# First FFN of a fused decoder kernel: the remainder of half of P on VectorE straight from PSUM, the scaling of X on ScalarE, and newly written instruction lists

## The reference, cut to what matters

```
x = layernorm(x + attention(x))                      # 16 heads, causal
x = layernorm(x + mixing(context, context, x))       # 16 heads of 8, a causal long convolution
x = layernorm(x + ffn0(x))                           # the part that the change touches
x = layernorm(x + state_space(x))                    # convolution, gated scan, RMS norm
x = layernorm(x + mixing1(x, context))
x = layernorm(x + ffn1(x))                           # ternary weights, Hadamard transform
```

```
xq = activation_quant(rms_norm(x))        # round(127 / max|x| * x), per token
g  = silu(xq @ sign(W_g).T)               # 256 -> 1024
u  = xq @ sign(W_u).T                     # 256 -> 1024
p  = g * u
y  = p @ sign(W_d).T                      # 1024 -> 256, p isn't quantised
```

## Time and profile before

| | us |
|---|---|
| runs | 695.28, 695.84, 696.39 |
| the profiled execution | 695.4 |
| its span (first to last instruction) | 693.3 |
| TensorE matmul busy | 668.4 (96%) |
| VectorE busy | 605.5 (87%) |
| GpSimd busy | 570.5 (82%) |
| ScalarE busy | 423.5 (61%) |

### The profile page before, as it was taken

The page is one execution under the profiler, slowest core; times in us unless marked ns, Lnnn a source line. Parts: engine busy times, 40 slices in busy tenths (PEclk is TensorE's granted clock), DMA queues, the critical chain, the costliest instruction groups (busy, mean ns, idle before and its releaser), DMA issues. The chain is left out here.

```text
span 693.3 us, 13904 instructions
## 1 busy us (share of the span) xinstructions
PE 668.4 (96%) x4318; PEld 482.1 (70%) x4318; DVE 605.5 (87%) x1329; ACT 423.5 (61%) x692; POOL 570.5 (82%) x750
## 2 busy tenths in 40 slices
PE   8999999999999899998899999999999999999994
PEld 7888888754444577786688888855444477777883
DVE  5988889679999998878899999889999998888774
ACT  1765666721370686976798888830101468888985
POOL 3986988987878699994467889999988989989952
PEclk9999999999999999999999999999999999999998
DMA  8820000000400050000211111122000000000001
GB/s 309 334 107 1 2 2 2 2 1 0 182 0 0 1 213 21 2 2 1 95 62 61 61 62 62 62 75 66 0 0 1 0 1 2 16 17 17 16 17 45
DMA packets 12726, 33.39 MB, mean 48 GB/s; under 512 B 2672, under 2 KB 8048, under 8 KB 11376
## 3 DMA queue, kind: packets, MB, share of 16 engines
q1 hardware_dynamic: 12080, 31.99, 12.5%
q10 hardware_dynamic: 576, 0.53, 0.3%
HBM read 30.35 MB, written 2.16 MB: 47 GB/s over the span
## 5 line engine op out<-in xcount | busy, mean ns | idle before, releaser
L1084 PE MATMUL bank<-XT,win_late 128*128 128x256 f32 x320 | 79.8, 385 | 2.0 <-DVE ss_xc L1269 1.6
L632 DVE TENSOR_REDUCE MIX<-m_pr 128x128 f32<-128x1024 f32 x64 | 76.6, 1206 | 0.4
L1269 DVE SCALAR_TENSOR_TENSOR ss_xc<-bank,cw_late,ss_xc 128x254 f32<-128x254 f32 x144 | 67.7, 477 | 6.2 <-ACT ss_xc L1173 2.7
L577 POOL TENSOR_TENSOR m_kv<-CTXT 128x512 f32<-128x512 f32 x64 | 65.1, 1042 | 7.4 <-PE bank L609 7.2
L577 POOL TENSOR_TENSOR m_kv<-XT,CTXT 128x512 f32<-128x512 f32 x64 | 68.0, 1089 | 1.4 <-PE bank L609 1.4
L607 PE MATMUL bank<-m_kv,toep 128*128 128x512 f32 x128 | 66.3, 600 | 1.2 <-POOL m_kv L577 1.0
L609 PE MATMUL bank<-m_kv,toep 128*128 128x512 f32 x128 | 65.4, 592 | 0.0
L608 PE MATMUL bank<-m_kv,toep 128*128 128x512 f32 x128 | 65.4, 592 | 0.0
L1084 PEld LDWEIGHTS bank<-XT,win_late 128*128 128x128 f32 x320 | 56.7, 190 | 11.9 <-DVE ss_xc L1269 4.3
L1562 PE MATMUL bank<-had_last,f_ht 128*128 128x256 f32 x256 | 59.4, 379 | 0.0
L445 POOL TENSOR_TENSOR at_p<-at_p,at_mx 128x512 f32<-128x512 f32 x44 | 45.0, 1041 | 10.6 <-DVE at_mx L355 10.5
(11 more groups left out here) (255 smaller groups left out, 1946.6 us busy)
## 6 DMA issues: line engine op xcount, KB each, us to landing
MIX<-cum_rows SPq DMA_DIRECT2D x15, 512.0 KB, 3.6
...
```

Source lines behind the costliest of these rows:

```text
L577: m = nc.gpsimd.tensor_tensor(KV[n % 3][:, c, :, :].rearrange("p (b j) i -> p b j i", b=HB), ki, vj, ALU.mult)
L632: nc.vector.tensor_reduce(head(MIX)[:, :, a, bass.ts(h, HB), :], PR[n % 2][:, :, :, :].rearrange("p c (b j) i -> p c b j i", b=HB), op=ALU ...
L1084: m = nc.tensor.matmul(bX[(NU * g + n) % 3][:, 0:GS_], win[:, h, off:off + P], XT[:, h, bass.ts(g, GS_)], start=(h == 0), stop=(h == C - 1))
L1269: m = nc.vector.scalar_tensor_tensor(acc[:, :, sh:S], bank[:, :, 0:S - sh], cw[:, r, n:n + 1], acc[:, :, sh:S], ALU.mult, ALU.add)
```

## The change

It has three parts.

1. The remainder of half 0 of P is computed by VectorE from PSUM: P in the bank minus the rounded P. ScalarE's copy of half 0 and GpSimd's subtraction of half 0 go; for half 1 both stay. The bank of half 0 comes free after VectorE's subtraction.
2. `lift` moves from VectorE to ScalarE as an activation with a scale and a bias column; GpSimd fills the bias column once.
3. All four lists are written anew, those of the attention, the mixers, the state space stage and the second FFN included. Apart from the parts above they hold the same calls.

```diff
-    PMT, = two("pmt", [P, FC, S], n=1)
+    PMT, = two("pmt", [P, FC // 2, S], n=1)
...
-    columns = ch.sb("f0_columns", [P, 26])
+    columns = ch.sb("f0_columns", [P, 27])
+    rnd = columns[:, 26:27]
...
             pe.wait_ge(s[f"p{k}_made"], n + 1)
-            upto(pe, s[f"p{k}_kept"], 2 * n)
+            upto(pe, s["p1_kept"], 2 * n) if k else upto(pe, s["p0_rest"], n)
...
             if low:
-                pe.wait_ge(s["p_rest"], 2 * n + k + 1)
+                pe.wait_ge(s[f"p{k}_rest"], n + 1)
             else:
-                pe.wait_ge(s[f"p{k}_kept"], 2 * n + 1)
+                pe.wait_ge(s[f"p{k}_kept"], 2 * n + 1 if k else n + 1)
...
-        def keep_p(n, k):
+        def keep_p(n):
...
+            act.wait_ge(s["p1_turned"], n + 1)
+            upto(act, s["p1_rest"], n)
+            nc.scalar.copy(PMT[:, :, :], bP[1][:, :].rearrange("p (r s) -> p r s", r=4)).then_inc(s["p1_kept"], 1)
+
+        def lift(n):
...
+            act.wait_ge(s["scaled"], 2 * n + 2)
+            upto(act, s["q_made"], n - 1)
+            nc.scalar.activation(Z[n % 2][:, :], X[:, n, :], ACT.Identity, scale=SC[n % 2][:, :], bias=rnd).then_inc(s["shifted"], 1)
...
-        def lift(n):
...
-            nc.vector.tensor_scalar(Z[n % 2][:, :], X[:, n, :], SC[n % 2][:, :], ROUND, ALU.mult, ALU.add).then_inc(s["shifted"], 1)
...
+        def rest_p(n):
...
+            dve.wait_ge(s["p0_kept"], n + 1)
+            upto(dve, s["downed"], 4 * n - 1)
+            nc.vector.tensor_tensor(PL[:, 0:4, :], bP[0][:, :].rearrange("p (r s) -> p r s", r=4), PH[:, 0:4, :].bitcast(F32),
+                                    ALU.subtract).then_inc(s["p0_rest"], 1)
...
+            if n == 0:
+                nc.gpsimd.memset(rnd, ROUND)
...
-        def rest_p(n, k):
...
-            pool.wait_ge(s[f"p{k}_kept"], 2 * n + 2)
-            upto(pool, s["downed"], 4 * n - 1 + k)
-            quarter = slice(4 * k, 4 * k + 4)
-            nc.gpsimd.tensor_tensor(PL[:, quarter, :], PMT[:, quarter, :], PH[:, quarter, :].bitcast(F32), ALU.subtract).then_inc(s["p_rest"], 1)
+        def rest_p(n):
...
+            pool.wait_ge(s["p1_kept"], 2 * n + 2)
+            upto(pool, s["downed"], 4 * n)
+            nc.gpsimd.tensor_tensor(PL[:, 4:8, :], PMT[:, :, :], PH[:, 4:8, :].bitcast(F32), ALU.subtract).then_inc(s["p1_rest"], 1)
...
 def gpsimd_order(a, m, f, x, n, g, again):
...
-    a.shift(1, 1); a.shift(1, 2); a.shift(1, 3); a.spread(3); a.shift(2, 0); a.shift(2, 1); a.shift(2, 2); a.shift(2, 3); a.shift(3, 0); a.spread(4)
...
+    a.shift(1, 1); a.shift(1, 2); a.shift(1, 3); a.spread(3); a.shift(2, 0); a.shift(2, 1); a.spread(4); a.shift(2, 2); a.shift(2, 3); a.residual(0)
```

More of the change, by code:

```diff
@@ L810, in round_p @@
             act.wait_ge(s[f"p{k}_turned"], n + 1)
-            upto(act, s["p_rest"], 2 * n - 1 + k if n else 0)
+            upto(act, s[f"p{k}_rest"], n)
             upto(act, s["downed"], 4 * n - 3 + k)
@@ L910, in norm_out @@
             norm(dve, nc, Y2[n % 2], X[:, n, :], MV3[n % 2], RS3[n % 2], s["rstd3"], s["normed3"], n)
[L912 to L913 removed]
+        return calls(add_x=add_x, stats=stats, aggregate=aggregate, norm_x=norm_x, peak=peak, step_size=step_size, quantise=quantise,
+                     multiply=multiply, rest_p=rest_p, add_down=add_down, stats3=stats3, norm_out=norm_out)
     def gpsimd(pool):
@@ new lines, in tensor_order @@
+    m.mix(5); a.context_turn(15); m.mix(6); a.x_turn(10); a.project(15); a.x_turn(11); m.mix(7); m.mix(8); a.x_turn(12); m.mix(9); a.x_turn(13)
+    m.mix(10); a.x_turn(14); m.mix(11); m.mix(12); a.x_turn(15); m.mix(13); m.mix(14); m.mix(15); m.mix(16); m.mix(17); m.mix(18); m.mix(19)
+    m.totals(); m.mix(20); f.mix_turn(0); m.mix(21); f.mix_turn(1); m.mix(22); m.mix(23); m.mix(24); f.mix_turn(2); m.mix(25); m.mix(26)
+    f.mix_turn(3); m.mix(27); m.mix(28); m.mix(29); m.mix(30); f.q_turn(0); m.mix(31); f.gate(0, 1); f.up(0, 1); f.mix_turn(4); f.gate(0, 0)
@@ new lines, in tensor_order @@
+    x.square_sum(14, 11); n.mix(8); x.x_turn(11, 15); x.out_product(14); n.mix(9); x.square_sum(15, 12); n.mix(10); x.x_turn(12, 16)
+    x.out_product(15); n.mix(11); n.mix(12); x.x_turn(13, 16); n.mix(13); x.x_turn(14, 16); n.mix(14); x.x_turn(15, 16); n.mix(15); n.mix(16)
+    n.mix(17); g.mix_turn(0); g.skip(0); n.mix(18); n.mix(19); g.mix_turn(1); g.skip(1); n.mix(20); n.mix(21); g.mix_turn(2); g.skip(2); n.mix(22)
+    n.mix(23); n.mix(24); g.q_turn(0); g.mix_turn(3); g.skip(3); n.mix(25); n.mix(26); n.mix(27); n.mix(28); g.gate(0, 0); g.up(0, 1); g.mix_turn(4)
@@ new lines, in tensor_order @@
+    g.up(0, 0); g.gate(0, 1); g.skip(4); g.q_turn(1); n.mix(29); g.gate(1, 0); g.up(1, 1); g.q_turn(2); g.up(1, 0); g.gate(1, 1); g.mix_turn(5)
+    g.skip(5); g.gate(2, 0); n.mix(30); g.up(2, 1); g.gate(2, 1); g.h_turn(0, 0); n.mix(31); g.q_turn(3); g.up(2, 0); g.transform(0, 0)
+    g.h_turn(0, 1); g.mix_turn(6); g.skip(6); g.gate(3, 0); g.transform(0, 1); g.h_turn(1, 0); g.q_turn(4); g.gate(3, 1); g.mix_turn(7); g.skip(7)
+    g.h_turn(1, 1); g.up(3, 0); g.transform(1, 0); g.transform(1, 1); g.w_turn(0); g.up(3, 1); g.gate(4, 0); g.h_turn(2, 0); g.gate(4, 1)
@@ L2174, in gpsimd_order @@
-    n.mix(26); n.mix(27); g.rstd(2); n.mix(28); g.rstd(3); g.edge(5); n.mix(29); n.mix(30); n.mix(31); g.first(0); g.edge(6); g.second(0); g.rstd(4)
-    g.edge(7); g.first(1); g.second(1); g.rstd(5); g.first(2); g.second(2); g.rstd(6); g.edge(8); g.rstd(7); g.first(3); g.second(3); g.edge(9)
-    g.first(4); g.edge(10); g.second(4); g.rstd3(0); g.rstd(8); g.first(5); g.rstd3(1); g.second(5); g.first(6); g.rstd(9); g.rstd3(2); g.edge(11)
-    g.second(6); g.rstd(10); g.first(7); g.second(7); g.rstd(11); g.edge(12); g.edge(13); g.rstd3(3); g.first(8); g.second(8); g.rstd(12); g.first(9)
@@ new lines, in gpsimd_order @@
+    g.rstd(2); n.mix(28); g.edge(5); n.mix(29); n.mix(30); n.mix(31); g.rstd(3); g.edge(6); g.first(0); g.second(0); g.edge(7); g.rstd(4); g.first(1)
+    g.second(1); g.edge(8); g.rstd(5); g.first(2); g.edge(9); g.second(2); g.rstd(6); g.rstd(7); g.first(3); g.second(3); g.first(4); g.second(4)
+    g.rstd(8); g.edge(10); g.first(5); g.rstd3(0); g.second(5); g.rstd(9); g.edge(11); g.first(6); g.edge(12); g.rstd3(1); g.second(6); g.rstd3(2)
+    g.first(7); g.rstd(10); g.second(7); g.rstd3(3); g.edge(13); g.first(8); g.rstd(11); g.second(8); g.first(9); g.rstd(12); g.second(9); g.rstd3(4)
@@ L2183 @@
+    g.edge(14); g.first(10); g.rstd(13); g.second(10); g.rstd3(5); g.edge(15); g.rstd3(6); g.rstd(14); g.first(11); g.second(11); g.rstd(15)
+    g.first(12); g.second(12); g.rstd3(7); g.first(13); g.second(13); g.rstd3(8); g.first(14); g.second(14); g.rstd3(9); g.rstd3(10); g.rstd3(11)
+    g.rstd3(12); g.rstd3(13); g.rstd3(14); g.rstd3(15)
 AT = ("wqk_in weights_in later_in pool_consts consts proj_in value_in out_in bv_spread bias_made bp_made "
```

622 lines of the change are left out of this document (300 added, 322 removed).

## The result

The changed kernel takes 727.45 us (median of 4, 726.65 to 728.37) against 695.56 on the same chip: a ratio of 1.0457, interval 1.0442 to 1.0473. The forecast was 699.6, range 695.2 to 703.0. The direction was right, the size was wrong by 28 us, and most of what was missed lies in stages for which the prediction had put down nothing. The profiled execution took 727.04 us, its span 725.1.

What follows compares the result with a forecast made beforehand. TensorE was taken to bound the first FFN, VectorE second. 4.9 us lost, less 1.1 recovered, plus 0 gave 3.8; on the profiled 695.4 that is 699.2, with 0.44 for the median 699.6, range 695.2 to 703.0.

Steps and rivals of the forecast that it cites:

- The other orders: Reordered lists outside the first FFN: 0 (0.8 either way) for attention's first scores, 1 us either way for state space.
- the seam: Start of the first FFN behind the mixer, at 226 to 232 us, where all other engines wait for ScalarE.
- The head of line on ScalarE: First FFN's start: four second-FFN weight instructions wait behind the first copy of Q, putting TensorE 4.9 us behind.
- for two such steps: First FFN's start: 0.42 us for two handovers between first Silu, VectorE's product and TensorE's first turn of P.
- the 1.1 taken off as recovered: First FFN: TensorE wins back half of some 2.15 us of its idle time, 1.1 us.
- The operations at nothing: First FFN: moved subtraction and scaling cost nothing beside TensorE's work; bounds 2.15 us gained, 5.1 lost.
- The moved hop of Q: First FFN: Q goes from VectorE to ScalarE and back, hidden because Q is turned a sample ahead of P.
- The relief wins: Rival, first FFN: relieving GpSimd wins 2.15 us and the start 0.8, giving 692.9 us; chance 0.15.
- lost and given back: Rival: 4.9 us lost at the first FFN's start is regained there and in state space, giving 695.9; chance 0.13.
- VectorE becomes the bound: Rival, first FFN: VectorE's added 5.1 us lie on the path, giving 705.8, or 703.3 for half; chance 0.12.
- the four instructions behind the copy: Sign on ScalarE: three of L549 and one of L556 stand behind the first copy of Q.
- 3 to 4 and over 1: Sign: TensorE idles 3 to 4 us before the first turn of P, over 1 before the next gate product.

Runs made afterwards that it cites:

- the first run: The kernel before with the change's first FFN (its operations and lists), all other stages in the order of before: 704.67 us, ratio 1.0142.

## Why the prediction was wrong

**The failed step** is "The other orders": "in the mixers and the second FFN TensorE has no gaps to win", "1 us either way for the state space stage", and 0 within 0.8 for the attention. An engine that is 97% busy has no gaps to win, but each call moved in four lists can open one. The runs put 2.7 (attention), 8.3 (state space stage) and 10.9 us (second FFN) there, 21.9 of 31.9. I had the first scores and the seam read call by call and had read nothing of the two stages that hold most of the rewritten lines. The idea was one-sided too: where TensorE is nearly full a rewriting can win little and lose much. What the new lists did there is known in part only. In the second FFN 7.2 of the 10.9 us were VectorE's sums stretched beside GpSimd and the late scale; 3.7 there, most of the 8.3 of the state space stage and the 2.7 of the attention stay without a cause that an experiment has shown. That the direction came out right is in part luck: the reason given for it carries some 7 of the 31.9 us.

**The head of line on ScalarE** was right in place and timing (8.05 and 11.19 us against 8.06 and 11.27) and mis-sized: 4.9 less 1.1 us forecast, 7.1 measured alone and 6.5 in the changed kernel. Three things are wrong in the term. The path: the first turn of P was taken to wait for the first Silu and VectorE's product (the 0.42 "for two such steps" rests on that), but it waits for the second Silu, whose bank it writes; so the four turns of P and a turn of the mixer's output came behind the wait in place of inside it, and the next gate product started at 242.61, 1.2 us behind the end of the second copy where 0.2 was forecast. TensorE's clock: the work behind the wait ran at 0.50, which is 1.6 us lost in the first run and 2.4 in the changed kernel by the traces. Before has no wait that long inside the program, so the term needed a rival at half clock. And the 1.1 taken off as recovered: the 5.6 us of waiting and 1.6 of clock in the first run make up the 7.1 without it. In the changed kernel the same count is 5.6 and 2.4, 8.0 against 6.5, so there some may have come back; the scatter of those runs doesn't let one say.

**The operations at nothing** was wrong for the lists of before (7.3 for both, 10.9 and 6.3 apart, where my bound for a loss was 5.1), and nearer where the lists were written for them (2.1 together with the rest of the stage's new order). The bound was VectorE's added busy time. The waits in the runs are those of calls that stand behind the added one in VectorE's queue: TensorE waits 9.6 us for the bank of the last product and for Q with the subtraction alone (1.6 for the bank in before). The moved hop of Q that I called hidden is a part of it: 3.3 us of TensorE's waits with the scaling alone.

**The rivals.** "The relief wins" and "lost and given back" are out: the stages after the first FFN only add to the loss. "VectorE becomes the bound" named the right engine for the operations in the old lists, and its 705.8 was still short of the changed kernel's 727.45. No rival said that the rewritten lists could be worse by themselves, although they were the largest part of the diff.

**The signs named in advance.** Right: the four instructions behind the copy, both times after it, GpSimd's fall of 20.4 us over the span (64.11 in the 100 us, near 67 forecast). Wrong: one wait of 5.92 in place of 3 to 4 and over 1; TensorE's idle time in the 100 us, 9.89 in place of near 7; VectorE's busy time there, 85.91 in place of near 94; and the sentence that I would be wrong "if the attention, the state space stage or the second FFN differ by more than 1.5 us" came true three times.
